# A fused four-stage kernel on one core: a new order of its head, with the mixed weights made in 32 products of 32 rows and 64 columns

## The chip, the cores and the metric

The kernel runs on one core of one Trainium2 chip. The metric is the device time of one execution in microseconds (us); the median of three runs is used.

## The reference, cut to what matters

The input x is [16 batches, 128, 128], and each batch has a row of 8 condition values, `cond_8`. Four residual stages follow one another:

```python
x = x + L0(x)   # per batch: one expert of 8 (argmax of cond), up/gate/down, silu, hidden 256
x = x + L1(x)   # base linear + 8 rank-16 adapters, mixed per batch by cond
x = x + L2(x)   # linear with w_bot[b] = sum_g cond[b, g] * weight[g] * mask, plus bias
x = x + L3(x)   # top-2 of 8 experts per batch (gelu, hidden 512), weighted, plus a shared expert
```

The linears of stages L1 and L2 depend on the batch through `cond_8` alone, so their 16 weight matrices per stage can be made before x is touched.

## The kernel before, in words

All work is written by hand per engine, with semaphores between the engines; each engine executes its own list in order.

**The head.** SP loads `cond_sb`, `lora_sb` and `w2_sb` (lines 258 to 260), ACT's queue loads `cond_rep` (cond repeated over the partitions), `small_sb` and x (385 to 387). TensorE (PE) first multiplies zeros (`warm`, 443 and 458). VectorE (DVE) finds the top 8 of each batch (632 to 637); a small product carries the first expert numbers to one row, `at_row` (461, 652), from which SP reads the addresses of the L0 experts and loads them into a ring of 10 slots (266). DVE makes `bs_w`, the adapters' second factor times cond (656), then `y_delta` (662), then works out by 26 small instructions, nearly all chained, which of 32 slots each (batch, expert) pair takes (`payload`, 667 to 707).

PE meanwhile makes the L1 weights: four products of 128 rows and 512 columns (`prepare1`, 452), which ACT copies out (397) and GpSimd (POOL) adds to the base weight (353, `lin1`). Then it makes the mixed L2 weights: 16 products of 64 rows and 128 columns (480), two of them side by side on the two halves of the array's rows; ACT copies them out in four pieces (402) and POOL multiplies by the mask in 16 pieces (361, `lin2`). Only then comes the first batch of stage L0 (`upgate0(0)`, 490), behind it a product that spreads `payload` over the partitions (508), which waits for all of ACT's copies, and then the other batches. DVE copies `slot_row` and `w_col` out of that product (722, 723), and SP and POOL wait for them (303, 348).

**The rest.** Each batch of L0 is 4 products for up and gate (490), silu on ACT (408), a multiply on DVE (714) and 2 products for down (498). After 16 batches come L1 and L2 for four groups (523, 530, and DVE's 735), and the split of x into a high part (ACT 414) and a low part (DVE 741). L3 then runs through a fixed list of units (`ORDER`); its weights are split into two parts by POOL first: the shared expert (365, 367) and then 12 pairs of slots ("duos", 375 and 378, three pieces each). All L3 products run as pairs of high and low parts (544, 554, 561, 588, 603, 612).

**Queues.** SP issues the ring loads, the shared expert's weights (300), the duo loads (272) and the solo loads (281) in one order; a ring slot is loaded again when its batch is done (265), a duo's raw buffer when POOL has split it (271).

Of the kernel before, what the change touches and what calls it, by code (L numbers as in the profile page):

```python
# [22 lines left out]
P = 128  # L23
B = 16
E = 8
# [21 lines left out]
HALF = P // 2  # L47
J = HALF // E
QUADS = 2
RANKED = 12  # L50
BASE1, MASK2, DELTA, BIAS1, BIAS2 = 0, P, 2 * P, 2 * P + J, 2 * P + J + 1
# [10 lines left out]
EYE, IOTA, EVENS, BELOW, EARLIER, NUMBER, SLOT = E, E + B, 2 * E + B, 2 * E + 2 * B, 2 * E + 2 * B + E * E, \  # L62
    2 * E + 3 * B + E * E, 2 * E + 3 * B + E * E + 1
COND = SLOT + SLOTS

SLOTS0 = 10
FREE = 2
PAIRS = 3
# [50 lines left out]
def build_kernel(nc, xT, cond, condT, lora, small, w2, experts0, experts3, shared, out):  # L119
    ctx = ExitStack()  # L120
    with ctx:
# [3 lines left out]
        def sem(name):  # L125
# [13 lines left out]
        w2_sb = sb("w2_sb", [P, E, P])  # L139
# [20 lines left out]
        pw_rest = sb("pw_rest", [B, K])  # L160
        pw_all = sb("pw_all", [B, K])
# [5 lines left out]
        reached = sb("reached", [B, E, B])  # L167
        even_odd = sb("even_odd", [B, 2, E])
        in_front = sb("in_front", [B, 2, E, E])
        starts = sb("starts", [B, 2, E])  # L170
        evens = sb("evens", [B, 1])
        even_slot = sb("even_slot", [B, E])
        odd_slot = sb("odd_slot", [B, E])
        is_odd = sb("is_odd", [B, E])
        shift = sb("shift", [B, E])
        shifted = sb("shifted", [B, E])
# [4 lines left out]
        payload = sb("payload", [B, 3, K, SLOTS])  # L181
        slot_row = sb("slot_row", [1, 2 * SLOTS], U32)
# [7 lines left out]
        mix_raw = sb("mix_raw", [P, QUADS, 2, GB, B, J])  # L190
# [25 lines left out]
        route = sem("route")  # L216
# [3 lines left out]
        chosen_done, rank_mm, payload_done, slots_mm, slots_done = (  # L220
            sem("chosen_done"), sem("rank_mm"), sem("payload_done"), sem("slots_mm"), sem("slots_done"))
        ydelta_done, bsw_done = sem("ydelta_done"), sem("bsw_done")
        prep_mm, prep_copied = sem("prep_mm"), sem("prep_copied")
# [33 lines left out]
        def _(sp):  # L257
            sp.dma_start(cond_sb[:, :], cond).then_inc(cond_in, 16)
            sp.dma_start(lora_sb[:, :], lora).then_inc(lora_in, 16)
            sp.dma_start(w2_sb[:, :, :], w2).then_inc(w2_in, 16)  # L260
# [45 lines left out]
            for b in range(SLOTS0 + 2, B):  # L306
                load0(b)
# [33 lines left out]
        def _(pool):  # L341
# [4 lines left out]

            pool.wait_ge(small_in, 16)
            pool.wait_ge(slots_done, 1)
            for q in range(G):
                pool.wait_ge(prep_copied, q + 1)  # L350
# [19 lines left out]
            for j in range(DUOS):  # L370
# [3 lines left out]
                for n in range(3):  # L374
                    pool.tensor_copy(duo_hi[:, j % HALVES, piece(n)], raw_duo[:, j % RAWS, piece(n)])\  # L375
# [66 lines left out]
        def _(pe):  # L442
# [26 lines left out]
            for q in range(G):  # L469
                prepare1(q)  # L470
# [417 lines left out]
```

## Time and profile before

| | us |
|---|---|
| median of three runs | 153.79 (153.7 to 154.18) |
| the profiled execution's own time | 154.21 |
| its span, first to last instruction | 152.2 |
| time around the span | 2.0 |

The profiled execution lies 0.42 us above the median of the runs. In the span PE is busy 97%, DVE 72%, POOL 61% and ACT 47%; the granted TensorE clock reads 1.00 of full speed on average.

In the rows, PE is a product, PEld a load of its weights, and SPq and ACTq are DMA issues on the queues of SP and ACT. L12 is line 12 of the kernel. An fp32 product leaves two records of a load and two of a product, so `x8` at line 490 are four products.

### The profile page before, as it was taken

To read this page: it belongs to the slowest core of one execution; us is meant where nothing else is said; L and a number is where in the kernel's file an instruction comes from. 1 tells how busy PE (TensorE), PEld (TensorE's weight loads), DVE (VectorE), ACT (ScalarE), POOL (GpSimd) and SP (SyncE) were. 2 spreads that over 40 slices of the span, in tenths; PEclk is the share of its full clock that TensorE was granted. 3 is DMA by queue.
4 is the path that set the end of the run, shared out by engine and by line. 5 is a ranking of instruction groups with operands and counts; after the bars stand their busy time and mean duration, and the time that the engine had idled before them with its cause. 6 is when DMAs were issued, how large, how long until landed. Compare 5 with 4: busy or idle time off the path is not lost.

```text
span 152.2 us, 3148 instructions
## 1 busy us (share of the span) xinstructions
PE 147.4 (97%) x1091; PEld 134.0 (88%) x1091; DVE 110.0 (72%) x229; ACT 71.6 (47%) x138; POOL 93.1 (61%) x101
## 2 busy tenths in 40 slices
PE   7999999999999999999999999999999999999992
PEld 2468999999976999899989999999989999999881
DVE  2984666666896686768875868876587886968772
ACT  3666444462374554544454354545425434346640
POOL 1002999999910006939994939995875999880000
PEclk9999999999999999999999999999999999999999
DMA  3999999971653667294297477086448047000052
GB/s 93 395 408 401 413 400 394 424 253 39 243 216 109 179 155 253 48 294 140 57 324 243 146 234 243 5 281 225 187 116 297 5 126 287 6 0 0 0 209 71
DMA packets 13919, 30.15 MB, mean 198 GB/s; under 512 B 1344, under 2 KB 8016, under 8 KB 13776
## 3 DMA queue, kind: packets, MB, share of 16 engines
q1 hardware_dynamic: 13472, 28.76, 54.4%
q10 hardware_dynamic: 432, 1.19, 2.2%
q8 instruction: 9, 0.15, 0.4%
q14 instruction: 6, 0.05, 0.2%
HBM read 24.71 MB, written 1.05 MB: 169 GB/s over the span
## 4 chain that ended last, share of the span: by engine, by line
PE 83%; DVE 7%; ACT 3%; POOL 3%; issue 2%; ACTq 0%; DVEq 0%; POOLq 0%
PE pair L554 21%; PE acc L603 10%; PE pair L544 9%; PE pair L490 9%; PE pair L561 8%; PE acc L588 6%; PE acc L498 5%; PE acc L612 5%; PE acc L445 3%; PE pair L452 2%; PE pair L523 2%; DVE hid L776 2%; DVE hid_lo L767 2%; POOL duo_lo L378 2%; DVE x_hl L741 2%; ACT hid_hi L438 2%
## 5 line engine op out<-in xcount | busy, mean ns | idle before, releaser
L378 POOL TENSOR_TENSOR duo_lo<-raw_duo,duo_hi 128x512 fp32r<-128x512 f32 x36 | 49.1, 1364 | 2.9
L767 DVE TENSOR_TENSOR hid_lo<-hid,hid_hi 128x512 fp32r<-128x512 f32 (+1 forms) x41 | 36.1, 883 | 17.8 <-ACT hid_hi L438 17.3
L438 ACT ACTIVATE hid_hi<-hid 128x512 fp32r<-128x512 f32 (+1 forms) x41 | 25.4, 622 | 44.0 <-DVE hid L776 41.1
L375 POOL CAST duo_hi<-raw_duo 128x512 fp32r<-128x512 f32 x36 | 28.4, 790 | 27.1 <-PE acc L603 27.1
L776 DVE TENSOR_TENSOR hid<-pair,act 128x512 f32<-128x512 f32 (+1 forms) x49 | 32.9, 673 | 5.6 <-PE pair L554 4.1
L554 PE MATMUL pair<-x_duo,duo_hi 128*128 128x256 f32 x192 | 35.1, 281 | 0.2 <-POOL duo_lo L378 0.2
L419 ACT ACTIVATE act<-pair 128x512 f32<-128x512 f32 x48 | 28.3, 590 | 9.6 <-PE pair L554 7.7
L554 PEld LDWEIGHTS pair<-x_duo,duo_hi 128*128 128x128 f32 x192 | 29.6, 188 | 0.9 <-issue 0.4
L554 PE MATMUL pair<-x_duo,duo_lo 128*128 128x256 f32 x96 | 26.8, 279 | 0.0
L544 PE MATMUL pair<-x_hl,shared_hi 128*128 128x512 f32 x64 | 20.5, 402 | 0.0
L554 PEld LDWEIGHTS pair<-x_duo,duo_lo 128*128 128x128 f32 x96 | 18.0, 188 | 0.0
L490 PE MATMUL pair<-x,ring 128*128 128x128 f32 x128 | 17.1, 277 | 0.0
L714 DVE SCALAR_TENSOR_TENSOR hid<-pair,ring,act 128x128 f32<-128x128 f32 x32 | 9.8, 346 | 8.5 <-PE pair L490 7.1
L490 PEld LDWEIGHTS pair<-x,ring 128*128 128x128 f32 x128 | 15.6, 192 | 0.2
L561 PE MATMUL pair<-x,raw_solo 128*128 x128 | 15.6, 275 | 0.0
L561 PEld LDWEIGHTS pair<-x,raw_solo 128*128 128x128 f32 x128 | 15.1, 192 | 0.3
L408 ACT ACTIVATE act<-pair,ring 128x128 f32<-128x128 f32 x32 | 10.0, 366 | 11.0 <-PE pair L490 11.0
L603 PE MATMUL acc<-hid_hi,duo_hi 128*128 128x256 f32 x48 | 14.2, 296 | 0.0
L603 PE MATMUL acc<-hid_hi,duo_lo 128*128 128x256 f32 x48 | 13.5, 282 | 0.0
L603 PE MATMUL acc<-hid_lo,duo_hi 128*128 128x256 f32 x48 | 13.5, 281 | 0.0
L544 PEld LDWEIGHTS pair<-x_hl,shared_hi 128*128 128x128 f32 x64 | 11.3, 189 | 2.0
L544 PE MATMUL pair<-x_hl,shared_lo 128*128 128x512 f32 x32 | 12.6, 394 | 0.0
(101 smaller groups left out, 200.6 us busy)
## 6 DMA issues: line engine op xcount, KB each, us to landing
raw_duo<-experts SPq DMA_DIRECT2D x12, 768.0 KB, 5.1
ring<-experts SPq DMA_DIRECT2D x16, 386.5 KB, 6.5
raw_solo<-experts SPq DMA_DIRECT2D x8, 768.0 KB, 4.7
x_duo<-x_hl SPq DMA_DIRECT2D x24, 128.0 KB, 3.8
x<-xT ACTq DMA_DIRECT2D x1, 1024.0 KB, 6.6
lora_raw<-x SPq DMA_DIRECT2D x4, 256.0 KB, 2.3
raw_solo<-shared SPq DMA_DIRECT2D x1, 768.0 KB, 10.9
out<-lora_raw SPq DMA_DIRECT2D x3, 256.0 KB, 3.1
```

The source lines that it names most:

```text
L375: pool.tensor_copy(duo_hi[:, j % HALVES, piece(n)], raw_duo[:, j % RAWS, piece(n)])\
L378: pool.tensor_tensor(duo_lo[:, j % HALVES, piece(n)], raw_duo[:, j % RAWS, piece(n)], duo_hi[:, j % HALVES, piece(n)].bitcast(F32), ALU.su ...
L408: act.activation(act0[:, b % FREE, c, :], pair[b % FREE][0][:, c * P:(c + 1) * P], ACT.Silu, bias=ring0[:, b % SLOTS0, BUP0 + c:BUP0 + c + ...
L419: act.activation(act3[:, u % PAIRS, :], pair[u % PAIRS][0][:, :], ACT.Gelu_apprx_tanh)\
L438: act.activation(hid_hi[:, k % SPLITS, at], hid3[:, u % PAIRS, at], ACT.Copy)\
L490: ins = pe.matmul(pair[b % FREE][half][:, c * P:(c + 1) * P], ring0[:, b % SLOTS0, base + c * P:base + (c + 1) * P], x[:, cols(b)], start= ...
L544: ins = pe.matmul(bank[:, :].rearrange("p (b n) -> p b n", n=P), w[:, at], x_hl[:, n * GB:(n + 1) * GB, h, :], start=(m == 0), stop=(m == 2))
L554: ins = pe.matmul(bank[:, i * N2:(i + 1) * N2], w[:, n % HALVES, at], x_duo[:, n % GATHERS, h, :], start=(m == 0), stop=(m == 2))
L561: ins = pe.matmul(bank[:, m * P:(m + 1) * P], raw_solo[:, n % RAWS, base + m * P:base + (m + 1) * P], x[:, cols(solo_batch[n])], start=Tru ...
L603: ins = pe.matmul(y, w[:, n % HALVES, at], v[:, k, i * N2:(i + 1) * N2], start=(part == 0 and i == 0 and m == 0), stop=(part == 1 and i == ...
L767: dve.tensor_tensor(hid_lo[:, k % SPLITS, at], hid3[:, u % PAIRS, at], hid_hi[:, k % SPLITS, at].bitcast(F32), ALU.subtract).then_inc(hid_ ...
L776: dve.tensor_tensor(hid3[:, u % PAIRS, at], pair[u % PAIRS][1][:, at], act3[:, u % PAIRS, at], ALU.mult).then_inc(mul_done, 1)
```

## The change

- **Loads.** `cond_rep` is no longer loaded: PE makes it from `cond_sb` with a small product (8 rows, 64 columns), ACT copies it out. `w2_sb` is loaded in two halves, ahead of x and `small_sb`, all on SP; ACT's queue keeps only `lora_sb`, behind a load of the exp table. `y_delta`'s pattern moves from `small_sb` into `w2_sb`.
- **DVE.** `y_delta` comes before `at_row`, and waits for the first half of `w2_sb`. The sorting takes a prefix sum and a predicated copy, fewer instructions, and comes behind `bs_w`. The weights of the top 2 are worked out on POOL.
- **PE.** Of eight `warm` products of 512 columns five are left, and two of 128 columns are added; the mixed L2 weights come before the L1 weights, as 32 products of 32 rows and 64 columns, four of them on the four quarters of the array's rows, into four banks. The `payload` product is one instead of two, and stands after `upgate0(3)`.
- **ACT.** Two of the four mixed banks are copied out before the L1 copies, and two between batches 0, 1 and 2 of L0.
- **POOL.** `lin1` and `lin2` no longer wait for `slots_done`; the mask takes 4 instructions of 512 elements in place of 16 of 128. The third piece of duo 1 waits for `hid_lo_done` 2.
- **SP.** The shared expert comes after 7 ring loads (10 before), and all ring loads come before the first duo.

The diff, cut to its core:

```diff
+TILES = 4
+ROWS = P // TILES
+J = ROWS // E
+KB = N // (B * J)
+MIXES = E // KB
+W2_HALF = J + E // 2 * P
...
-        prep = pair[2] + acc[:1]
-        mix = [[acc[1], pair[1][0]], [pair[1][1], pair[2][1]]]
-        cond_in, rep_in, lora_in = sem("cond_in"), sem("rep_in"), sem("lora_in")
-        small_in, w2_in = sem("small_in"), sem("w2_in")
+        prep = acc + pair[1]
+        mix = pair[1] + pair[2]
...
-            sp.dma_start(lora_sb[:, :], lora).then_inc(lora_in, 16)
-            sp.dma_start(w2_sb[:, :, :], w2).then_inc(w2_in, 16)
+            sp.dma_start(w2_sb[:, 0:W2_HALF], w2[:, 0:W2_HALF]).then_inc(w2_in[0], 16)
+            sp.dma_start(w2_sb[:, W2_HALF:], w2[:, W2_HALF:]).then_inc(w2_in[1], 16)
+            sp.dma_start(x[:, :], xT).then_inc(x_in, 16)
+            sp.dma_start(small_sb[:, :], small).then_inc(small_in, 16)
...
-            for b in range(4, SLOTS0):
-                load0(b)
-            sp.dma_start(shared_sb, shared).then_inc(shared_in, 16)
-            for b in range(SLOTS0, SLOTS0 + 2):
+            for b in range(4, B):
+                if b == SLOTS0 - 3:
+                    sp.dma_start(shared_sb, shared).then_inc(shared_in, 16)
                 load0(b)
             sp.wait_ge(slots_done, 1)
             duo_expert = values(mybir.EngineType.SP, slot_row[0:1, SLOTS:SLOTS + 2 * DUOS], E)
             load_duo(0)
...
+            pool.wait_ge(placed_done, 3)
+            pool.tensor_tensor(payload_sum[:, :, :], payload[:, :, 0, :], payload[:, :, 1, :], ALU.add)\
+                .then_inc(payload_done, 1)
...
-            for n in range(QUADS):
-                for h in range(2):
-                    pool.wait_ge(prep_copied, G + 2 * n + h + 1)
-                    for k in range(GB):
-                        at = (n * GB + k) * R + h * J
-                        mask = small_sb[:, MASK2 + at:MASK2 + at + J].unsqueeze(1).to_broadcast([P, B, J])
-                        ins = pool.tensor_tensor(lin2[:, :, at:at + J], mix_raw[:, n, h, k, :, :], mask, ALU.mult)
-                    ins.then_inc(lin2_done, 1)
+            for i in range(MIXES * TILES):
+                n, h = i // TILES, i % TILES
+                pool.wait_ge(mix_copied, i + 1)
+                at = slice(n * KB, (n + 1) * KB)
+                dst = lin2[:, :, :].rearrange("p b (k h j) -> p h k b j", h=TILES, j=J)[:, h, at, :, :]
+                mask = small_sb[:, MASK2:MASK2 + P].rearrange("p (k h j) -> p h k j", h=TILES, j=J)[:, h, at, :]
+                pool.tensor_tensor(dst, mix_raw[:, n, h, :, :, :], mask.unsqueeze(2).to_broadcast([P, KB, B, J]),
+                                   ALU.mult).then_inc(lin2_done, 1)
...
+                    if j == 1 and n == 2:
+                        pool.wait_ge(hid_lo_done, 2)
...
-            rep = condT.unsqueeze(1).to_broadcast([2 * E, J, B])
-            act.dma_start(cond_rep[:, :], rep).then_inc(rep_in, 16)
-            act.dma_start(small_sb[:, :], small).then_inc(small_in, 16)
-            act.dma_start(x[:, :], xT).then_inc(x_in, 16)
+            act.preload_act_table(ACT.Exp)
+            act.dma_start(lora_sb[:, :], lora).then_inc(lora_in, 16)
...
+            act.wait_ge(ydelta_done, 1)
+            act.activation(cond_rep[:, :], pair[0][0][:, 0:B * J].rearrange("p (b j) -> p b j", j=J)[:, :, 0],
+                           ACT.Copy).then_inc(rep_done, 1)
             act.preload_act_table(ACT.Silu)
+            def mixed(i):
+                n, h = i // TILES, i % TILES
+                act.wait_ge(mix_mm, n + 1)
+                act.activation(mix_raw[:, n, h, :, :, :].rearrange("p k b j -> p (k b j)"), mix[i][:, :], ACT.Copy)\
+                   .then_inc(mix_copied, 1)
+            mixed(0)
+            mixed(1)
             for q in range(G):
                 act.wait_ge(prep_mm, q + 1)
-                act.activation(lora_raw[:, q * GB:(q + 1) * GB, :].rearrange("p b o -> p (b o)"), prep[q % 3][:, :],
-                               ACT.Copy).then_inc(prep_copied, 1)
-            for n in range(QUADS):
-                act.wait_ge(prep_mm, G + n + 1)
-                for h in range(2):
-                    act.activation(mix_raw[:, n, h, :, :, :].rearrange("p k b j -> p (k b j)"), mix[n][h][:, :],
-                                   ACT.Copy).then_inc(prep_copied, 1)
+                act.activation(lora_raw[:, q * GB:(q + 1) * GB, :].rearrange("p b o -> p (b o)"), prep[q][:, :],
+                               ACT.Copy).then_inc(lora_copied, 1)
...
+                if b < 2:
+                    mixed(2 + b)
...
             pe.wait_ge(zeros_set, 1)
-            warm(5)
+            warm(3)
+            warm(1, P)
+            pe.wait_ge(cond_in, 16)
+            pe.matmul(pair[0][0][:, 0:B * J].rearrange("p (b j) -> p b j", j=J), cond_sb[0:E, OF:OF + P],
+                      cond_sb[0:E, TURNED:TURNED + B].unsqueeze(2).to_broadcast([E, B, J]), start=True, stop=True)\
+              .then_inc(rep_mm, 1)
+            warm(1, P)
             pe.wait_ge(ones_set, 3)
             pe.wait_ge(at_diag_done, 1)
             pe.matmul(acc[1][:, 0:B], ones_b[:, :], at_diag[:, :], start=True, stop=True).then_inc(at_mm, 1)
             warm(1)
             pe.wait_ge(chosen_done, 1)
             pe.matmul(pair[0][1][0:B, 0:E], earlier_b[:, :], chosen_b[:, :], start=True, stop=True)
             pe.matmul(pair[0][1][0:B, E:2 * E], ones_b[:, 0:B], chosen_b[:, :], start=True, stop=True)\
               .then_inc(rank_mm, 1)
-            warm(2)
+            warm(1)
+            pe.wait_ge(ydelta_done, 1)
+            for k in range(E):
+                if k % (E // 2) == 0:
+                    pe.wait_ge(w2_in[k // (E // 2)], 16)
+                for h in range(TILES):
+                    rows = slice(h * ROWS, (h + 1) * ROWS)
+                    ins = pe.matmul(mix[k // KB * TILES + h][:, k % KB * B * J:(k % KB + 1) * B * J],
+                                    w2_sb[rows, J + k * P:J + (k + 1) * P],
+                                    y_delta[rows, :, :].rearrange("p b j -> p (b j)"), start=True, stop=True)
+                if k % KB == KB - 1:
+                    ins.then_inc(mix_mm, 1)
             for q in range(G):
-                prepare1(q)
-            pe.wait_ge(ydelta_done, 1)
-            pe.wait_ge(w2_in, 16)
-            for n in range(QUADS):
-                if n:
-                    pe.wait_ge(prep_copied, 2)
-                for k in range(GB):
-                    for h in range(2):
-                        rows = slice(h * HALF, (h + 1) * HALF)
-                        ins = pe.matmul(mix[n][h][:, k * P:(k + 1) * P], w2_sb[rows, n * GB + k, :],
-                                        y_delta[rows, :, :].rearrange("p b j -> p (b j)"), start=True, stop=True)
-                ins.then_inc(prep_mm, 1)
+                pe.wait_ge(bsw_done, q + 1)
+                if q >= FREE:
+                    pe.wait_ge(mix_copied, q - FREE + 1)
+                pe.matmul(prep[q][:, :], lora_sb[:, AS1:AS1 + P],
+                          bs_w[:, q * GB:(q + 1) * GB, :].rearrange("p b o -> p (b o)"),
+                          start=True, stop=True).then_inc(prep_mm, 1)
...
-            pe.wait_ge(route, RANKED)
+            pe.wait_ge(rank_done, 1)
             upgate0(0)
-            pe.wait_ge(payload_done, 3)
-            pe.wait_ge(prep_copied, 2 * QUADS + G)
-            for k in range(K):
-                ins = pe.matmul(prep[0][:, 0:3 * SLOTS].rearrange("p (v s) -> p v s", v=3), ones[:, :],
-                                payload[:, :, k, :], start=(k == 0), stop=(k == K - 1))
-            ins.then_inc(slots_mm, 1)
+            pe.wait_ge(lora_copied, G)
             for b in range(B):
                 if b + 1 < B:
                     upgate0(b + 1)
-                if b == FREE:
+                if b == SORTED:
+                    pe.wait_ge(payload_done, 1)
+                    pe.wait_ge(mix_copied, 3)
+                    pe.matmul(pair[2][0][:, 0:3 * SLOTS], ones[:, :], payload_sum[:, :, :].rearrange("b v s -> b (v s)"),
+                              start=True, stop=True).then_inc(slots_mm, 1)
+                if b == SORTED + FREE:
                     pe.wait_ge(slots_done, 2)
...
+            dve.wait_ge(rep_mm, 1)
+            dve.wait_ge(w2_in[0], 16)
+            dve.tensor_tensor(y_delta[:, :, :], pair[0][0][:, 0:B * J].rearrange("p (b j) -> p b j", j=J),
+                              w2_sb[:, 0:J].unsqueeze(1).to_broadcast([P, B, J]), ALU.mult).then_inc(ydelta_done, 1)
             dve.wait_ge(at_mm, 1)
             dve.tensor_copy(at_row[:, :], acc[1][0:1, 0:B]).then_inc(at_done, 1)
+            dve.tensor_tensor(onehot[:, :, :], top_at[:, 0:K].unsqueeze(2).to_broadcast([B, K, E]),
+                              cond_sb[:, IOTA:IOTA + E].unsqueeze(1).to_broadcast([B, K, E]), ALU.is_equal)\
+               .then_inc(onehot_done, 1)
+            dve.wait_ge(onehot_done, 1)
+            dve.tensor_tensor(chosen_b[:, :], onehot[:, 0, :], onehot[:, 1, :], ALU.add).then_inc(chosen_done, 1)
+            dve.wait_ge(rank_mm, 1)
+            dve.tensor_copy(count_i[:, :], pair[0][1][0:B, E:2 * E]).then_inc(route, 1)
+            dve.tensor_copy(rank_n[:, :], pair[0][1][0:B, 0:2 * E]).then_inc(rank_done, 1)
+            dve.wait_ge(exp_done, 1)
+            dve.reciprocal(inv[:, 0:1], expsum[:, :]).then_inc(inv_done, 1)
+            dve.wait_ge(rep_done, 1)
...
+            dve.tensor_tensor_scan(starts[:, :], parts[:, 0:2 * E], none[:, :], 0.0, ALU.add, ALU.add).then_inc(route, 1)
...
-            dve.wait_ge(slots_mm, 1)
-            dve.tensor_copy(slot_row[:, :], prep[0][0:1, 0:2 * SLOTS]).then_inc(slots_done, 1)
-            dve.tensor_copy(w_col[:, :], prep[0][:, 2 * SLOTS:3 * SLOTS]).then_inc(slots_done, 1)
             for b in range(B):
                 if b + 1 < B:
                     hidden0(b + 1)
+                if b == SORTED:
+                    dve.wait_ge(slots_mm, 1)
+                    dve.tensor_copy(slot_row[:, :], pair[2][0][0:1, 0:2 * SLOTS]).then_inc(slots_done, 1)
+                    dve.tensor_copy(w_col[:, :], pair[2][0][:, 2 * SLOTS:3 * SLOTS]).then_inc(slots_done, 1)
```

## Rows read from the trace of the kernel before

**Rows 1.** The page, busy time of each engine (share of the span) xinstructions

```profile
PE 147.4 (97%) x1091; PEld 134.0 (88%) x1091; DVE 110.0 (72%) x229; ACT 71.6 (47%) x138; POOL 93.1 (61%) x101
```

**Rows 2.** Busy time by stretch: length, then each engine (instructions), clock, DMA share, GB/s

```profile
20.00:30.00 10.00, 10.00 (x92) 10.00 (x92) 6.54 (x23) 4.70 (x16) 9.92 (x16) 1.00 1.03 409
```

**Rows 3.** Chain that ended last, in order of time: start us, us, what

```profile
4.25 0.97 PE acc L445 x2
...
10.79 2.08 ACT mix_raw L402 x4
...
13.00 0.65 PE pair L508 x4
13.65 1.09 PE pair L490 x8
14.74 0.45 PE acc L498 x4
15.19 0.89 PE pair L490 x8
```

**Rows 4.** Timeline of the head, DVE and SP: start us, us, what [idle before]

```profile
3.39 0.15 DVE L649 TENSOR_TENSOR chosen_b<-onehot 16x8 bf16<-16x8 f32 x1
...
3.69 0.16 DVE L652 CAST at_row<-acc 1x16 uint32<-1x16 f32 x1 [0.15 <-PE acc L461]
3.78 2.48 DVE L656 SCALAR_TENSOR_TENSOR bs_w<-lora_sb,cond_rep 128x512 f32<-128x512 f32 x4
...
4.58 5.85 SPq L266 DMA_DIRECT2D ring<-experts  x10
...
6.19 0.27 DVE L662 TENSOR_TENSOR y_delta<-cond_rep,small_sb 128x128 f32<-128x128 f32 x1
```

**Rows 5.** DMA issues: out<-in, count, KB each, us from issue to landing

```profile
x<-xT ACTq DMA_DIRECT2D x1, 1024.0 KB, 6.6
...
w_sb<-w SPq DMA_DIRECT2D x1, 512.0 KB, 3.9
...
lora_sb<-lora SPq DMA_DIRECT2D x1, 128.0 KB, 2.3
```

**Rows 6.** Timeline of the L1 products, loads and products of one record each, line 452

```profile
5.86 0.34 PEld L452 LDWEIGHTS pair<-bs_w,lora_sb 128*128 128x128 f32 x1 [0.52 <-DVE bs_w L656]
...
6.71 0.34 PEld L452 LDWEIGHTS pair<-bs_w,lora_sb 128*128 128x128 f32 x1 [0.52 <-issue]
...
7.34 0.19 PEld L452 LDWEIGHTS acc<-bs_w,lora_sb 128*128 128x128 f32 x1 [0.29 <-issue]
...
7.77 0.19 PEld L452 LDWEIGHTS acc<-bs_w,lora_sb 128*128 128x128 f32 x1 [0.24 <-issue]
```

**Rows 7.** Timeline of the mixing products (L480) and of the loads behind payload's (L508)

```profile
10.02 0.27 PE L480 MATMUL acc<-y_delta,w_sb 64*128 64x128 f32 x1
...
10.13 0.27 PE L480 MATMUL acc<-y_delta,w_sb 64*128 64x128 f32 x1
...
13.19 0.30 PEld L508 LDWEIGHTS pair<-payload,ones 16*128 16x128 f32 x2
13.30 0.19 PEld L508 LDWEIGHTS pair<-payload,ones 16*128 16x128 f32 x1
```

**Rows 8.** Timeline of POOL's masks and splits, and of DVE's low parts

```profile
14.12 2.50 POOL L353 TENSOR_TENSOR lin<-lora_raw,small_sb 128x512 f32<-128x512 f32 x2 [11.31 <-DVE w_col L723]
...
19.03 6.68 POOL L361 TENSOR_TENSOR lin<-mix_raw,small_sb 128x128 f32<-128x128 f32 x16
...
27.19 3.45 POOL L367 TENSOR_TENSOR shared_lo<-raw_solo,shared_hi 128x1536 fp32r<-128x1536 f32 x1
...
40.78 0.68 DVE L741 TENSOR_TENSOR x_hl<-x,x_hl 128x512 fp32r<-128x512 f32 x1
40.82 1.79 POOL L378 TENSOR_TENSOR duo_lo<-raw_duo,duo_hi 128x512 fp32r<-128x512 f32 x1
...
42.04 1.12 DVE L741 TENSOR_TENSOR x_hl<-x,x_hl 128x512 fp32r<-128x512 f32 x1
```

More of the change, by code:

```diff
@@ L116, with build_kernel @@
 SUMMED = dict(zip(ORDER, itertools.accumulate(additions(unit) for unit in ORDER)))
-def build_kernel(nc, xT, cond, condT, lora, small, w2, experts0, experts3, shared, out):
+def build_kernel(nc, xT, cond, lora, small, w2, experts0, experts3, shared, out):
     ctx = ExitStack()
@@ L138, in build_kernel @@
         small_sb = sb("small_sb", [P, SMALL])
-        w2_sb = sb("w2_sb", [P, E, P])
+        w2_sb = sb("w2_sb", [P, J + E * P])
         shared_sb = raw_solo[:, 0, :]
@@ L166, in build_kernel @@
         rank_n = sb("rank_n", [B, 2 * E])
[L167 to L176, printed above, removed]
+        count_i = sb("count_i", [B, E], U32)
+        odd_i = sb("odd_i", [B, E], U32)
+        parts = sb("parts", [B, 2 * E + 1])
+        none = sb("none", [B, 2 * E])
+        starts = sb("starts", [B, 2 * E])
+        is_odd = sb("is_odd", [B, E], U32)
         slot_e = sb("slot_e", [B, E])
@@ L305, in _ @@
             load_duo(0)
-            for b in range(SLOTS0 + 2, B):
-                load0(b)
             load_duo(1)
@@ L345, in _, with weighed @@
             pool.tensor_copy(earlier_b[:, :], cond_sb[:, EARLIER:EARLIER + B]).then_inc(ones_set, 1)
+            step = [0]
+            def weighed(ins):
+                step[0] += 1
+                ins.then_inc(weigh, 1)
+                pool.wait_ge(weigh, step[0])
+            pool.wait_ge(inv_done, 1)
+            weighed(pool.tensor_scalar(probs[:, :], expd[:, 0:K], inv[:, 0:1], None, ALU.mult))
+            pool.tensor_tensor(pair_sum[:, :], probs[:, 0:1], probs[:, 1:2], ALU.add).then_inc(pair_done, 1)
+            pool.wait_ge(inv_done, 2)
+            weighed(pool.tensor_scalar(pw[:, :], probs[:, :], inv[:, 1:2], None, ALU.mult))
+            weighed(pool.tensor_scalar(pw_rest[:, :], pw[:, :], 1.0 - W_SCALE, None, ALU.mult))
+            weighed(pool.tensor_scalar(pw_part[:, :], pw[:, :], W_SCALE, None, ALU.mult))
+            weighed(pool.tensor_tensor(pw_all[:, :], pw_part[:, :], pw_rest[:, :], ALU.add))
+            pool.wait_ge(placed_done, 1)
+            weighed(pool.tensor_tensor(payload[:, 2, :, :], placed[:, :, :],
+                                       pw_all[:, :].unsqueeze(2).to_broadcast([B, K, SLOTS]), ALU.mult))
+            pool.wait_ge(placed_done, 3)
+            pool.tensor_tensor(payload_sum[:, :, :], payload[:, :, 0, :], payload[:, :, 1, :], ALU.add)\
+                .then_inc(payload_done, 1)
             pool.wait_ge(small_in, 16)
-            pool.wait_ge(slots_done, 1)
             for q in range(G):
-                pool.wait_ge(prep_copied, q + 1)
+                pool.wait_ge(lora_copied, q + 1)
                 base = small_sb[:, BASE1:BASE1 + P].unsqueeze(1).to_broadcast([P, GB, P])
@@ L432, in _ @@
                     if k >= SPLITS:
-                        act.wait_ge(down_done, [AT[x] for x in SPLIT_AT][k - SPLITS] + 1)
+                        act.wait_ge(down_done, [AT[other] for other in SPLIT_AT][k - SPLITS] + 1)
                     width = N // splits(unit)
@@ L442, in _, with warm @@
         def _(pe):
-            def warm(times):
+            def warm(times, columns=N):
                 for _ in range(times):
-                    pe.matmul(acc[0][:, :].rearrange("p (b n) -> p b n", n=P), zeros[:, :],
-                              zeros[:, :].unsqueeze(1).to_broadcast([P, GB, P]), start=True, stop=True)
-            def prepare1(q):
-                pe.wait_ge(bsw_done, q + 1)
-                if q >= len(prep):
-                    pe.wait_ge(prep_copied, q - len(prep) + 1)
-                pe.matmul(prep[q % 3][:, :], lora_sb[:, AS1:AS1 + P],
-                          bs_w[:, q * GB:(q + 1) * GB, :].rearrange("p b o -> p (b o)"),
-                          start=True, stop=True).then_inc(prep_mm, 1)
-            pe.wait_ge(zeros_set, 1)
-            warm(5)
+                    pe.matmul(acc[0][:, 0:columns].rearrange("p (b n) -> p b n", n=P), zeros[:, :],
+                              zeros[:, :].unsqueeze(1).to_broadcast([P, columns // P, P]), start=True, stop=True)
+            pe.wait_ge(zeros_set, 1)
+            warm(3)
[5 more added lines that the diff above has]
+            warm(1, P)
             pe.wait_ge(ones_set, 3)
@@ L690, in _ @@
-            chained(dve.tensor_tensor(even_slot[:, :], starts[:, 0, :], rank, ALU.add))
-            chained(dve.tensor_scalar(odd_slot[:, :], starts[:, 1, :], evens[:, 0:1], None, ALU.add))
-            chained(dve.tensor_tensor(is_odd[:, :], rank, even_odd[:, 0, :], ALU.is_ge))
-            chained(dve.tensor_tensor(shift[:, :], odd_slot[:, :], even_slot[:, :], ALU.subtract))
-            chained(dve.tensor_tensor(shifted[:, :], shift[:, :], is_odd[:, :], ALU.mult))
-            chained(dve.tensor_tensor(slot_e[:, :], even_slot[:, :], shifted[:, :], ALU.add))
@@ new lines, in _ @@
+            dve.tensor_tensor(is_odd[:, :], rank_n[:, 0:E], parts[:, 1:E + 1], ALU.is_ge).then_inc(route, 1)
+            dve.wait_ge(route, 8)
+            dve.tensor_tensor(slot_e[:, :], starts[:, 0:E], rank_n[:, 0:E], ALU.add).then_inc(route, 1)
+            dve.wait_ge(route, 10)
+            dve.copy_predicated(slot_e[:, :], is_odd[:, :], starts[:, E:2 * E]).then_inc(route, 1)
+            dve.wait_ge(route, 11)
+            dve.tensor_tensor(slot_ke[:, :, :], onehot[:, :, :], slot_e[:, :].unsqueeze(1).to_broadcast([B, K, E]),
+                              ALU.mult).then_inc(route, 1)
```

115 lines of the change are left out of this document (49 added, 66 removed).

## The prediction

> **What bounds the kernel now.** I read four views. The page's busy time comes first: the reader should see that TensorE is busy 97% of the span [rows 1]. The table by stretch then says where it is full: between 20 and 30 us PE is busy all 10.00 us, with the DMA engines full beside it at 409 GB/s [rows 2]. So what counts is when the unbroken stream of products begins. The chain in order of time gives that: ACT's four copies of the mixed weights hold it from 10.79 to 12.87, the `payload` product follows at 13.00, and from 13.65, the second batch of L0, the chain stays on PE, batch behind batch [rows 3]. Last, the timeline of the head tells what feeds it [rows 4, 6, 7]. A batch costs 0.89 for up and gate and 0.45 for down, 1.34 us together [rows 3]. Whatever lets the second batch begin earlier than 13.65 should come off the end, if the loads and POOL keep up.
>
> **Part by part: the new head on PE.**
>
> *Start of the mixing.* `y_delta` now waits for the first half of `w2_sb`. No row shows a half load. The nearest are `lora_sb`, 128 KB, issued second on SP at 1.23 and landed 2.3 later, at 3.5, and the whole `w_sb`, issued at 1.68 and landed 3.9 later, at 5.6 [rows 5]. Those are the bounds; in between 512 KB took 2.1 us, so 258 KB land near 4.0, which I take. `y_delta` is at most 0.27, `at_row` 0.16, `chosen_b` 0.15 and `onehot` about the same [rows 4]: `chosen_b` is ready near 4.8 instead of 3.54. One warm product (two took 0.97 [rows 3]) and the two rank products, some 0.1 by an estimate from `payload`'s steps in rows 7, put the first mixing product at 5.4. By the bounds it is 4.9 or 7.0.
>
> Behind that wait `at_row` ends near 4.4 instead of 3.85, and SP's first ring load goes out near 5.1 instead of 4.58 [rows 4]. I cost that at nothing: the same DMA engines are still busy with `w2_sb` and x until then, and x landed at 8.7 [rows 5].
>
> *The clock.* The granted clock reads 1.00 in the tables, but the spacing of equal records tells more: line 452's loads stand 0.85 apart from 5.86 to 6.71, 0.63 from there to 7.34, and 0.43 to 7.77 [rows 6]. That is 1.2 GHz up to about 7.0, and 2.4 GHz from there, after PE had worked almost from the start of the span with hardly a gap. I take the same moment for the new head.
>
> *The mixing.* Each of its records needs its own weights. Two tiles side by side advance one record every 0.11 (10.02 to 10.13) with 128 columns; the `payload` product, with 16 rows and only 96 columns, still loads every 0.11 (13.19 to 13.30) [rows 7]. So fewer rows and fewer columns did not shorten a step there. The old mixing has 16 such steps (8 products of 2 records, two tiles at a time), the new one 16 as well (8 of 2 records, four tiles at a time). I take 0.11 at 2.4 GHz and, from rows 6, twice that at 1.2. The bounds are 0.055 if 64 columns set the step, and 0.22 if four quarters load only two at a time. From 5.4 to 7.0 that makes 7.6 steps, and the other 8.4 take 0.9: the mixing ends at 7.9. The saving is its place, not its length.
>
> The Trainium skill agrees on the load (TensorE: Matmul & The Clock Gate, section LDWEIGHTS): it counts columns of the weights, so 32 rows of 128 columns take as long as 128 rows.
>
> *Behind it.* Four L1 products of 2 x 0.43 end at 11.35. DVE's four `bs_w`, 0.62 each, begin near 5.5 and are done by 8.0, one ahead of each product. ACT's copies, 0.52 apart where they follow one another (four in 2.08 [rows 3]), run two mixed, then four L1, from 8.1; the last starts behind the last L1 product and ends by 12.1. `upgate0(0)`, 0.89, ends at 12.25; so ACT's copies no longer stand on the path. The `payload` product, one of two records instead of two of two, costs 0.22. The stream is thus where it was at 13.65 by about 12.45: **1.2 us** earlier.
>
> **What I cost at nothing.** ACT's last two mixed copies, 0.52 each, stand between batches 0 to 2, where ACT is less than half busy (4.70 of 10.00 us [rows 2]). Were this cover gone, they would cost up to 1.0. DVE's 13 sorting instructions, near 0.2 each with their steps (0.15 to 0.16 long [rows 4]), and POOL's eight are done by about 11.5, and are now needed only after `upgate0(3)`, near 15. x and the first ring slot land by about 9.7, before 11.35. The ring loads take 0.97 each (396 KB at 409 GB/s [rows 2]) against 1.34 of work, and with the shared expert (1.9) ahead of the eighth, that lands near 18.4 and is needed at 20.7. The duos go out later on SP, behind all 16 ring loads, but arrive near 27, when POOL has just finished: its `lin1` is 5.0 (four of 1.25) from about 12, `lin2` between 5.0 (four at that size) and 6.7 (as before), the shared split 4.9 [rows 8], so 28.6 at the latest. POOL was first at its duos at 30.6.
>
> **The step to L3.** In the old run a low part on DVE takes 1.12 from 42.04, another of the same shape 0.68, and the long one ends 0.55 after POOL's last split of duo 1, which itself ran 1.79 until 42.6 [rows 8]. The two kept each other waiting. The new wait moves that split behind `hid_lo` 2, so DVE is free: **0.4 us**. If POOL is late after all, this is 0. Behind POOL's new wait stands its third piece of duo 1, and on SP the load of duo 3, both used several units later.
>
> **The sum.** 1.2 + 0.4 = 1.6 us. The profiled execution, 154.21 (152.2 of span and 2.0 around it), would become 152.6. It lies 0.42 above the median of the runs; from 153.79 the forecast is **152.2 us**.
>
> **Rivals.**
>
> *The columns set the step.* With 64 columns and four quarters at work, a step may take 0.11 at the lower clock and 0.055 at the higher. Then the mixing ends at 7.1, 0.8 earlier, and the time is 151.4. For it: with 128 columns load and columns cannot be told apart. Against it: the 96-column product at 0.11 [rows 7]. If the clock is up already at 5.4 as well, the mixing ends at 6.3 and the time is 150.6. The Trainium skill's page TensorEngine Tiling (Array Packing), Theoretical Speedup, has up to 4x for 32 rows against 2x for 64, which would halve the old 1.76 us of mixing to 0.88.
>
> *The clock rises later (slower).* The new head has three 512-column warm products fewer, it leaves PE idle near 4.0 to 4.8, and its mixing, if the loads pace it, streams only part of the time. If PE stays at 1.2 GHz, the mixing ends at 8.8 and each L1 product takes 1.71. With two of them at that rate the stream is at its old point at 15.0 instead of 13.65; less 0.4, that is 1.0 slower, 154.8; with all four it is 156.5. Each us by which the clock rises later costs 0.5 us, so the gain of 1.6 is gone if it rises after about 10.2. For it: PE needed until 7.0 with its denser start [rows 6]. Against it: most of the stretch from 5.4 on is still work.
>
> *Four quarters do not load together.* Then there are 32 steps of 0.11, the mixing ends at 9.7, and 1.8 of time is added to a gain of 1.6: 154.0. Against it: the old two halves share a step of 0.11 [rows 7].
>
> **How the numbers follow.** Forecast 0.45, columns 0.28, clock 0.18, loads apart 0.09. A measurement of this kernel can tell about 0.3%, 0.46 us, from no change. The first two are faster: 0.73. Of the clock's 0.18, 0.05 lies within 0.46, and most of the third: 0.11 the same; 0.16 slower. The range reaches from 150.8, which leaves out only the earliest clock, to 154.0, which leaves out the clock's dearer ends and some of the third. The forecast's own range is 151.8 to 152.9: a later half load costs up to 0.9, and the 0.4 may be missing.
>
> **What would show it.** Right: `mix` starts near 5.4 and advances one round of four tiles per 0.21, then 0.11; the records of the L1 products are 0.43 apart; the second batch of L0 begins near 12.2; L741 takes 0.68 four times; PE has no new gap from 15 to 34. Wrong: rounds of 0.055 or 0.22; L1 records 0.85 apart behind the mixing; a PE wait on `e0_in`, on `shared_done` or on ACT's copies; or a stream that begins earlier and still ends at the same time.

## The result, and the profile after

The changed kernel takes **156.83 us** (median of 4, 156.18 to 157.29) against 153.75 before (153.69 to 154.18). The ratio is 1.020, 95% interval 1.016 to 1.024: 3.1 us slower, where 152.2 was forecast and 154.0 was the upper end. The profiled execution took 156.54, with a span of 154.8 and 1.7 around it; that span is 2.6 longer than before.

The page, busy time of each engine (share of the span, instructions), answers to [rows 1]:

```profile
PE 149.9 (97%) x1122; PEld 136.4 (88%) x1122; DVE 109.1 (70%) x221; ACT 71.6 (46%) x139; POOL 94.7 (61%) x97
```

PE's share is the same 97%, so it has no new idle time: it is busy 2.5 us longer. The chain that ended last, in order of time (start us, us, what), shows where. It answers to [rows 3]; the mixing is now L506, the L1 weights L516, up and gate of L0 L526, the `payload` product L548, the linears of L1 L560:

```profile
4.04 0.23 DVE y_delta L681
...
5.39 3.62 PE pair L506 x64
9.02 3.71 PE acc L516 x4
12.73 1.97 PE pair L516 x4
14.70 1.85 PE pair L526 x16
...
19.23 0.39 PE pair L548 x2
19.62 0.64 PE acc L534 x4
...
37.10 3.57 PE pair L560 x32
...
45.76 0.69 DVE hid L803
...
51.54 1.31 DVE hid_lo L794
...
57.36 0.72 PE acc L640 x6
```

Three marks of the same chain of the kernel before, for the same work (first linear, first multiply of L3 on DVE, first down product of a duo):

```profile
34.71 3.57 PE pair L523 x32
...
43.75 0.68 DVE hid L776
...
54.95 0.71 PE acc L603 x6
```

The loss is complete where the linears begin: 37.10 against 34.71, 2.4 us. At DVE's first multiply of L3 it is 2.0, and at the first duo's down product 2.4 again. (The two traced executions are 2.3 us apart in time, the medians 3.1: the traced kernel before lies 0.4 above its median, the traced changed kernel 0.3 below.)

The timeline of the changed kernel, loads of the L1 weights as in [rows 6], then POOL and DVE at the step to L3 as in [rows 8]:

```profile
11.67 0.34 PEld L516 LDWEIGHTS pair<-bs_w,lora_sb 128*128 128x128 f32 x1 [0.52 <-issue]
12.52 0.34 PEld L516 LDWEIGHTS pair<-bs_w,lora_sb 128*128 128x128 f32 x1 [0.52 <-issue]
13.25 0.19 PEld L516 LDWEIGHTS pair<-bs_w,lora_sb 128*128 128x128 f32 x1 [0.39 <-issue]
13.68 0.19 PEld L516 LDWEIGHTS pair<-bs_w,lora_sb 128*128 128x128 f32 x1 [0.24 <-issue]
...
33.30 0.61 POOL L403 CAST duo_hi<-raw_duo 128x512 fp32r<-128x512 f32 x1 [7.12 <-DMA raw_duo<-experts]
...
49.55 0.69 DVE L794 TENSOR_TENSOR hid_lo<-hid,hid_hi 128x512 fp32r<-128x512 f32 x1 [0.70 <-ACT hid_hi L472]
...
51.00 1.29 POOL L406 TENSOR_TENSOR duo_lo<-raw_duo,duo_hi 128x512 fp32r<-128x512 f32 x1
...
51.54 1.30 DVE L794 TENSOR_TENSOR hid_lo<-hid,hid_hi 128x512 fp32r<-128x512 f32 x1 [0.70 <-ACT hid_hi L472]
```

The loads stand 0.85 apart up to 12.52 and 0.43 from 13.25: TensorE works at 1.2 GHz until about 13, where before it was at 2.4 GHz from about 7 [rows 6]. The whole mixing (16 rounds of 0.21), four of the eight L1 records and most of the fifth ran at the lower level. The granted clock reads 1.00 in all these stretches; only the spacing shows it.

### The profile page after: what moved, and what is told of

Its sections match the earlier page's. It is cut to its first block, busy times and chain, and to the rows that moved or that the text cites. A ratio compares the mean times of both kernels' runs of the same rounds, so it can differ in the third digit from the quotient of the medians.

```text
span 154.8 us, 3205 instructions
## 1 busy us (share of the span) xinstructions
PE 149.9 (97%) x1122; PEld 136.4 (88%) x1122; DVE 109.1 (70%) x221; ACT 71.6 (46%) x139; POOL 94.7 (61%) x97
## 4 chain that ended last, share of the span: by engine, by line
PE 83%; DVE 9%; ACT 2%; DMA 2%; issue 1%; SPq 0%; ACTq 0%; DVEq 0%
PE pair L591 21%; PE acc L640 10%; PE pair L526 9%; PE pair L598 9%; PE pair L581 8%; PE acc L625 5%; PE acc L534 5%; PE acc L649 5%; DVE hid L803 3%; DVE hid_lo L794 3%; PE acc L516 2%; ACT hid_hi L472 2%; PE pair L506 2%; PE pair L560 2%; DMA w_sb<-w 2%
## 5 line engine op out<-in xcount | busy, mean ns | idle before, releaser
L794 DVE TENSOR_TENSOR hid_lo<-hid,hid_hi 128x512 fp32r<-128x512 f32 (+1 forms) x41 | 38.6, 943 | 17.7 <-ACT hid_hi L472 17.3
L403 POOL CAST duo_hi<-raw_duo 128x512 fp32r<-128x512 f32 x36 | 29.1, 808 | 34.4 <-PE acc L640 19.9
L406 POOL TENSOR_TENSOR duo_lo<-raw_duo,duo_hi 128x512 fp32r<-128x512 f32 x36 | 48.2, 1338 | 2.9
L740 DVE SCALAR_TENSOR_TENSOR hid<-pair,ring,act 128x128 f32<-128x128 f32 x32 | 9.8, 347 | 13.1 <-PE pair L526 12.8
L526 PE MATMUL pair<-x,ring 128*128 128x128 f32 x128 | 16.8, 275 | 0.0
L526 PEld LDWEIGHTS pair<-x,ring 128*128 128x128 f32 x128 | 15.6, 192 | 0.5 <-issue 0.5
```

Of the source, the lines that this page charges most:

```text
L406: pool.tensor_tensor(duo_lo[:, j % HALVES, piece(n)], raw_duo[:, j % RAWS, piece(n)], duo_hi[:, j % HALVES, piece(n)].bitcast(F32), ALU.su ...
L526: ins = pe.matmul(pair[b % FREE][half][:, c * P:(c + 1) * P], ring0[:, b % SLOTS0, base + c * P:base + (c + 1) * P], x[:, cols(b)], start= ...
L794: dve.tensor_tensor(hid_lo[:, k % SPLITS, at], hid3[:, u % PAIRS, at], hid_hi[:, k % SPLITS, at].bitcast(F32), ALU.subtract).then_inc(hid_ ...
```

## The experiments

Three theories. **Form**: the mixing's products of 64 columns stream too little, and stand where the clock should rise. **Warm**: the missing warm products and the gaps ahead of 5.3 hold it down. **Steps**: the clock apart, only the number of steps counts.

The moment at which the clock rises is read from the spacing of the L1 or mixing records: one spacing lies between the two levels, and it is divided in proportion.

| run | products ahead of the full clock | 1.2 GHz until about | linears begin | median | ratio to before |
|---|---|---|---|---|---|
| before | 8 warm, L1 | 7.1 | 34.71 | 153.75 | |
| changed | 5 + 2 short warm, 64-column mixing, L1 | 13.1 | 37.10 | 156.83 | 1.020 |
| `e1_two_halves` | as changed, 128-column mixing | 8.4 | 34.92 | 155.13 | 1.0105 (1.0071 to 1.0138) |
| `e2_no_gaps` | 8 warm, 64-column mixing, L1 | 13.4 | 37.45 | 157.06 | 1.0229 (1.0199 to 1.026) |
| `e3_l1_first` | as changed, L1 ahead of the mixing | 8.9 | 35.95 | 155.96 | 1.0155 (1.0112 to 1.0197) |
| `e4_before_three_warm_fewer` | 5 warm, L1 | 8.5 | 35.11 | 154.28 | 1.0051 (1.0025 to 1.0077) |
| `e7_halves_64_columns` | as changed, 64-column mixing in 64 rows | 18 | 41.30 | 160.56 | 1.0438 (1.0387 to 1.049) |

Each ratio is to runs of the kernel before on the same chip (medians 153.4 to 153.7).

**Two halves again** (`e1_two_halves`, `e8_two_halves_again`):

```diff
-TILES = 4
+TILES = 2
```

> The changed kernel with one number changed: the mixed weights come from 16 products of 64 rows and 128 columns, two tiles side by side, in the new order and with the new few warm products. In the changed kernel the L1 products' records stand 0.85 us apart up to 12.5, and the clock is up only near 13.1; before it was near 7.0. Theory 'form' (products of 64 columns stream too little to bring the clock up): here the records of the mixing are full again, the clock rises near 7 to 9, the L1 products follow at 0.43, and the median falls by 2 to 3 us, to about 154. Theory 'warm' (the missing warm products and the gaps before 5.3 hold the clock down): no change, the clock still rises near 13 and the median stays near 156.8. Theory 'cost of the products alone' (clock as it is, only the number of steps counts): 16 steps as before, no change.

Timeline, loads of the mixing (L506) and of the L1 weights (L516):

```profile
5.38 3.32 PEld L506 LDWEIGHTS pair<-y_delta,w_sb 64*128 64x128 f32 x32 [0.44 <-issue]
8.82 0.30 PEld L516 LDWEIGHTS acc<-bs_w,lora_sb 128*128 128x128 f32 x2
9.35 0.19 PEld L516 LDWEIGHTS acc<-bs_w,lora_sb 128*128 128x128 f32 x1 [0.24 <-issue]
9.78 0.19 PEld L516 LDWEIGHTS acc<-bs_w,lora_sb 128*128 128x128 f32 x1 [0.24 <-issue]
```

One number changed, and the L1 products run 0.43 apart; the linears begin 2.2 earlier than in the changed kernel, and the median is 1.7 lower, a little less than expected. So *form*, not *warm* or *steps*. The mixing itself took nearly the same time (3.4 us instead of 3.6): the step stayed at 0.21 and fell to 0.11 only for its last two, when the clock rose near 8.4. That is still later than the 7.1 of the kernel before, which stays ahead.

> The kernel with two halves once more, for a second look at its clock, since its six times lie between 154.29 and 155.81. If the clock rises at another moment in another execution, this trace shows it at another place than near 8.8, and its time differs by about half of that shift; if the clock rises at the same place, the spread has another cause.

The loads are 0.43 apart from 9.91 on, the clock rises near 9.5 instead of 8.4, and the span is 0.5 longer (153.1 against 152.6), about half of the shift. The moment moves between executions and the time with it.

**No gaps** (`e2_no_gaps`), full warm products ahead of the mixing:

```diff
-            warm(3)
-            warm(1, P)
+            warm(4)
...
-            warm(1, P)
+            warm(1)
...
-            warm(1)
+            warm(2)
             pe.wait_ge(chosen_done, 1)
```

> The changed kernel with warm products of 512 columns in its three gaps before 5.3 us (eight of 512 columns in all, as in the kernel before), the mixing still 32 products of 64 columns. Theory 'warm': the clock rises near 7, the mixing's rounds of four go from 0.21 to something shorter, the L1 products run at 0.43 apart, and the median falls by 2 to 3 us. Theory 'form': the clock still rises near 13, the median stays within 0.5 us of 156.8.

Timeline, loads of the L1 weights:

```profile
12.93 0.34 PEld L515 LDWEIGHTS pair<-bs_w,lora_sb 128*128 128x128 f32 x1 [0.52 <-issue]
13.60 0.19 PEld L515 LDWEIGHTS pair<-bs_w,lora_sb 128*128 128x128 f32 x1 [0.33 <-issue]
14.03 0.19 PEld L515 LDWEIGHTS pair<-bs_w,lora_sb 128*128 128x128 f32 x1 [0.24 <-issue]
```

Eight warm products do not help: the clock is as late as in the changed kernel. *Warm* falls for the changed kernel.

**L1 first** (`e3_l1_first`): the loop over the L1 products stands ahead of the mixing loop, ACT's copies in the same order, `prep = acc + pair[0]`.

> The changed kernel with the four L1 products ahead of the 32 mixing products (banks and copies follow), all else as changed. Theory 'form': from 5.7 on PE streams 512 columns per record again, so the clock rises near 7 to 10, and the mixing then runs at 2.4 GHz: its round of four takes 0.11 us if the loads set it, 0.055 if the columns do. The median falls by 1.5 to 3 us. Theory 'warm': the clock rises as late as in the changed kernel, near 13, and L1 products and mixing take 1.71 and 0.21 again; median near 156.8 or above.

Timeline, the L1 weights (L504), then the mixing (L514):

```profile
5.92 1.22 PE L504 MATMUL acc<-bs_w,lora_sb 128*128 128x512 f32 x1 [0.45 <-DVE bs_w L700]
...
8.65 0.32 PEld L504 LDWEIGHTS pair<-bs_w,lora_sb 128*128 128x128 f32 x1 [0.52 <-issue]
9.21 0.19 PEld L504 LDWEIGHTS pair<-bs_w,lora_sb 128*128 128x128 f32 x1 [0.24 <-issue]
...
11.02 2.01 PE L514 MATMUL pair<-y_delta,w_sb 32*128 32x64 f32 x64
```

With 512-column products from 5.9 on the clock is up near 9. The mixing takes 2.0 us at 2.4 GHz for 16 rounds, as the old form did. The median falls by 0.9 only, less than expected. The L1 products wait for `bs_w` until 5.92, where those of the kernel before began at 5.00. ACT's two mixed copies also hold back the second batch, by about 0.3: its products could have followed at 13.95 and began at 14.23.

**Fewer warm products before** (`e4_before_three_warm_fewer`): `warm(5)` to `warm(3)`, `warm(2)` to `warm(1)`.

> The kernel before with five warm products of 512 columns instead of eight (three of the first five, one of the last two), nothing else. Theory 'warm': the clock rises later than 7.0, the L1 products take 1.71 longer, and the time grows by 1 to 3 us. Theory 'form': the L1 products, which start near 4.8, bring the clock up near 7 to 8.5 all the same; the time stays within 0.5 us of 153.75.

Timeline, loads of the L1 weights:

```profile
7.88 0.34 PEld L452 LDWEIGHTS acc<-bs_w,lora_sb 128*128 128x128 f32 x1 [0.52 <-issue]
8.60 0.19 PEld L452 LDWEIGHTS pair<-bs_w,lora_sb 128*128 128x128 f32 x1 [0.39 <-issue]
9.03 0.19 PEld L452 LDWEIGHTS pair<-bs_w,lora_sb 128*128 128x128 f32 x1 [0.24 <-issue]
```

The clock comes near 8.5, about 1.4 later, and the median is 0.6 to 0.8 higher, between the two expectations. Where full products follow, warm products do count, though for a fifth to a quarter of the loss.

**Columns or tiles** (`e7_halves_64_columns`): on top of two halves,

```diff
+                    for c in range(2):
+                        at = k % KB * B * J + c * B // 2 * J
```

with 64 columns per product.

> The kernel with two tiles of 64 rows, but each of its 16 products cut into two of 64 columns: 32 products, 64 columns as in the changed kernel, 64 rows as in the kernel with two halves. Theory 'columns' (products of 64 columns leave the array half empty between two loads): 32 steps of 0.21 at the lower clock, 6.9 us of mixing, the clock still down at its end and up only some us into the L1 products; the median is 3 us or more above the changed kernel's 156.8. Theory 'tiles' (it is the four tiles of 32 rows that keep the clock down): the clock rises near 9 as with two halves, the rest of the mixing runs at 0.11, and the median lies between 155 and 157.5.

Timeline, the mixing (L508), then loads of the L1 weights (L519):

```profile
5.42 7.15 PE L508 MATMUL pair<-y_delta,w_sb 64*128 64x64 f32 x64
...
16.92 0.34 PEld L519 LDWEIGHTS pair<-bs_w,lora_sb 128*128 128x128 f32 x1 [0.52 <-issue]
17.78 0.29 PEld L519 LDWEIGHTS pair<-bs_w,lora_sb 128*128 128x128 f32 x1 [0.52 <-issue]
18.31 0.19 PEld L529 LDWEIGHTS pair<-x,ring 128*128 128x128 f32 x1 [0.24 <-issue]
```

With the tiles of `e1_two_halves` and only the columns halved, 32 steps of 0.22 run at 1.2 GHz from end to end, and the clock is up near 18. So the 64 columns are enough to keep the clock down, without tiles of 32 rows: the step is as long with 64 columns as with 128 (0.22 and 0.21), and carries half as many. Whether tiles of 32 rows with more columns would do it too was not tried.

**The titled part alone, in the old place** (`e12_before_four_quarters`): the kernel before with 32 products of 32 rows and 64 columns behind its L1 products.

> The kernel before with the titled part of the change alone: in the old place, behind the L1 products, the mixed weights come from 32 products of 32 rows and 64 columns, four quarters of the rows side by side, and POOL's mask in four instructions. Theory 'the load sets the step': at 2.4 GHz 16 rounds of four, 0.11 each, 1.8 us as before; ACT's four copies can start only behind the last product, 0.5 to 0.7 later than before, so the payload product and the stream move by as much: 0.4 to 0.8 us slower than the kernel before. Theory 'columns set the step': 0.055 a round, 0.9 us of mixing, and the time is 0.1 to 0.5 us below the kernel before. If the clock falls again during the thin mixing: 1 us or more slower.

Timeline, one tile's products:

```profile
8.74 0.27 PE L475 MATMUL acc<-y_delta,w_sb 32*128 32x64 f32 x1
...
8.86 0.27 PE L475 MATMUL acc<-y_delta,w_sb 32*128 32x64 f32 x1
```

Chain in order of time:

```profile
10.66 2.07 ACT mix_raw L399 x4
...
12.87 0.65 PE pair L503 x4
```

A round of four takes 0.11, and 16 rounds 1.9: no shorter, no longer. The clock, already up near 5.3 in this execution, did not fall. Median 153.44 against 153.53, ratio 0.9993 (0.9968 to 1.0018): unchanged. The cost of ACT's later copies is there in the trace: from the first mixing product (8.58) to the `payload` product (12.87) it is 4.29, against 3.42 in the kernel before, 0.9 more. In this execution the earlier clock hides it (linears at 34.59 against 34.71); why the median does not show it stays open. So the 32 products did harm only where they preceded the full clock.

**POOL's wait** (`e5_no_pool_wait`): `pool.wait_ge(hid_lo_done, 2)` left out.

> The changed kernel without POOL's new wait for hid_lo 2 (the third piece of duo 1 is split as soon as its buffer is there). Theory 'moved stall' (the wait only moves the collision of POOL and DVE, from the low parts of x near 44 to the third hid_lo at 51.5, which took 1.30 instead of 0.69): POOL's third piece runs at about 42.9 to 44.8, one low part on DVE takes about 1.1, the hid_lo takes 0.69 again, and the median stays within 0.5 us of 156.8. Theory 'the wait helps': 0.4 us or more slower. Theory 'the wait hurts' (it is part of the 3 us): 0.5 us or more faster.

Timeline, POOL's third piece of duo 1 and DVE:

```profile
44.69 1.30 POOL L404 TENSOR_TENSOR duo_lo<-raw_duo,duo_hi 128x512 fp32r<-128x512 f32 x1
...
44.72 1.81 DVE L766 TENSOR_TENSOR x_hl<-x,x_hl 128x512 fp32r<-128x512 f32 x1
...
52.89 0.69 DVE L792 TENSOR_TENSOR hid_lo<-hid,hid_hi 128x512 fp32r<-128x512 f32 x1 [0.70 <-ACT hid_hi L470]
```

157.04, ratio 1.0198 (1.0145 to 1.025): no change from the changed kernel's 1.020. The collision is a low part of x again (1.81, done 0.54 after POOL's split beside it), and the third `hid_lo` is back at 0.69: the wait only chose the victim. The Trainium skill (Advanced Engine Details and Errata, VectorE Performance Modes, its note on the second Vector SBUF port) says that this port is shared with GpSimd, and that GpSimd instructions and Vector instructions that use two ports block each other. Whether DVE's subtraction is one of those no run shows; that it is held up beside POOL's split the rows do show.

**Versions meant to beat both.** `e6_l1_first_dense`: L1 first, `bs_w` made earlier, 512-column warm products in the gaps, the mixed banks away from batches 0 and 1.

> A version meant to beat both: the changed kernel with the L1 products first again, their bs_w made earlier (about 4.0 instead of 5.1), 512-column warm products in the gaps before them, then the 32 mixing products, in banks that keep ACT's copies off batches 0 and 1. Theory 'form': the clock is up near 7, the L1 products end near 9.5, the mixing takes 1.8 (16 steps of 0.11), the second batch starts near 12.4 instead of 13.65, the payload product costs 0.6 in the stream, and the median is about 0.5 to 0.8 below the kernel before, near 153.0. Theory 'warm or place': if the clock is late here too, it is 155 or more.

154.85, ratio 1.0074 (1.0046 to 1.0103): slower than the kernel before. Its loads turn from 0.85 to 0.43 apart between 8.62 and 9.31, not near 7, though PE is busy from 1.0. Ahead of its L1 products it has one warm product fewer than the kernel before (seven), and the small product of `cond_rep` at 2.8; whether either is the cause was not tried.

`e9_before_copies_off_path`: the kernel before with the mixed banks in `acc` and `pair[2]`, two of ACT's copies between batches, the `payload` product after `upgate0(3)`.

> The kernel before, its dense start and its order of the products kept, with two things of the changed kernel that do not touch the clock: the mixed weights go to banks that batches 0 and 1 do not need, with two of ACT's four copies between those batches, and the payload product stands after upgate0(3); POOL's lin1 waits for the payload instead of slots_done. Theory: the clock rises near 7 as before, the second batch starts near 12.5 instead of 13.65, the payload product (two products here) costs about 0.6 to 0.8 in the stream, and the median falls by 0.3 to 0.6 us. If the head's gain is given back elsewhere: within 0.3 us of the kernel before.

Timeline, the L1 products (L456) and the mixing (L484), then the chain in order of time:

```profile
4.69 3.60 PE L456 MATMUL pair<-bs_w,lora_sb 128*128 128x512 f32 x8
8.22 1.05 PE L484 MATMUL acc<-y_delta,w_sb 64*128 64x128 f32 x14
```

```profile
33.27 3.57 PE pair L532 x32
...
48.01 0.79 issue
48.80 1.64 PE pair L563 x12
...
54.65 0.71 PE acc L612 x6
```

The median is 153.84 against 153.62, ratio 1.0011 (0.9982 to 1.0039): no gain. The linears begin 1.4 earlier than in the trace of the kernel before, but that is hardly the edit's doing. In this execution the clock was up near 4.4 instead of 7.1, and all eight L1 records took 3.6. From the first mixing product to the linears it is 25.05 (8.22 to 33.27), against 25.13 before (9.58 to 34.71): the copies off the path gained about 0.9, and the `payload` product cost about 0.8 in the stream. At the first duo's down product the 1.4 has become 0.3, because PE waits 0.79 ahead of that duo's products. The wait is for the gather of x: the second of its two copies was issued at 45.24 and landed at 48.71, and the product began at 48.80; POOL's splits for this duo were long done.

`e11_copies_off_path_pool_wait`: the same with POOL's wait.

> The kernel before with ACT's copies off the path (as in the run of that name, where the products of L1 began at 33.27 instead of 34.71 but the first duo waited 0.79 at 48.0 and nothing was left in the time), and with the changed kernel's wait of POOL's third piece of duo 1 for hid_lo 2. Theory 'both bounds': the low part of x that took 1.15 takes 0.68, the gather of x for the first duo goes out 0.4 earlier, and the median falls to 0.3 to 0.5 us below the kernel before. Theory 'the collision moves': the third hid_lo takes 1.3 and gives the 0.4 back; within 0.3 us of the kernel before.

153.67, ratio 1.0009 (0.9986 to 1.0032). The wait ahead of the first duo is 0.90 there, and ends the same way (copy landed at 48.38, product at 48.47). No version was faster than the kernel before.

**The changed kernel again** (`e10_changed_again`):

> The changed kernel once more, one look. If its spread (156.18 to 157.29) is the moment at which the clock rises, the records of the L1 products turn from 0.85 to 0.43 apart at another place than near 13.1, and the time moves by about half the shift. In no case should the clock be up before the mixing ends near 9.

Timeline, loads of the L1 weights:

```profile
11.72 0.34 PEld L516 LDWEIGHTS pair<-bs_w,lora_sb 128*128 128x128 f32 x1 [0.52 <-issue]
12.57 0.19 PEld L516 LDWEIGHTS pair<-bs_w,lora_sb 128*128 128x128 f32 x1 [0.52 <-issue]
13.01 0.19 PEld L516 LDWEIGHTS pair<-bs_w,lora_sb 128*128 128x128 f32 x1 [0.24 <-issue]
```

The spacing turns at 12.57 instead of near 13.1, and the linears begin at 36.86 instead of 37.10: half of the shift, as expected. The whole span is only 0.1 shorter (154.7 against 154.8), so the spread of the times has other causes too.

## Why the prediction was wrong, step by step

**The step that failed is the clock**: "I take the same moment for the new head". PE stayed at 1.2 GHz until about 13 instead of 7. The mixing ended at 9.0 instead of 7.9, and the four L1 products took 5.7 instead of 3.44: 3.3 us. The rival "the clock rises later" had this, with its place and its cause ("its mixing, if the loads pace it, streams only part of the time"). I gave it 0.18, because "most of the stretch from 5.4 on is still work". That was the mistake: I had just worked out that the load sets the step and that fewer columns do not shorten it, and still counted steps with half of the columns as full work.

The rival's price was 154.8 for two L1 products at the lower level and 156.5 for four. About two and a half came, which is 155.2 by that price; the measured 156.8 is more, mainly for three reasons that follow: the `payload` product, the traces against the medians, and the step to L3.

**The `payload` product** was sized at 0.22. In the stream it costs 0.39 and makes the down product behind it 0.64 instead of 0.45: 0.58 in all, 0.36 more.

With these two terms the forecast at the linears, 1.2 earlier, becomes 1.2 - 3.3 - 0.36 = 2.5 later; measured 2.4.

**The trace that the forecast was read from** had a late clock. Of four traces with the head of the kernel before, it rises near 7.1 in this one and near 5.3, 4.4 and 4.2 in `e12_before_four_quarters`, `e9_before_copies_off_path` and `e11_copies_off_path_pool_wait`; and the execution lies 0.4 above its median. So the medians are further apart (3.1) than the two traces (2.3).

**The step to L3.** The 0.4 came as forecast: the low part that took 1.12 [rows 8] ran in 0.69, and the loss at DVE's first multiply of L3 is 2.0 instead of 2.4. It was given back six us later, where the third `hid_lo` takes 1.30 beside POOL's moved piece. I had looked at what the piece delays on POOL and on SP, not at what it meets on DVE.

**The premise of the sum**, that what begins earlier "should come off the end", holds only in part: where the stream ran 1.4 earlier (`e9_before_copies_off_path`) the gain shrank to 0.3 at the first duo, which waited for its gather of x. Whether the 1.2 would have come off in full with the clock as I took it, no run shows.

**What was right.** The half load landed at 3.9 (forecast 4.0), the mixing began at 5.33 (5.4). A round takes 0.21 at 1.2 GHz, and 0.11 at 2.4 (`e3_l1_first`, `e12_before_four_quarters`): the load sets it, so the rivals "columns" and "four quarters do not load together" both fall. Up to 4x for 32 rows, as the Trainium skill has it (TensorEngine Tiling (Array Packing), Theoretical Speedup), shows in no run here: at 2.4 GHz, from the first record to the product behind, 64 records of 32 rows took 1.94 us (`e3_l1_first`), and 32 records of 64 rows 1.99 in the kernel before. ACT's copies and the sorting left the path, and PE has no gap between 15 and 34. POOL was at its duos later than I had it (33.3, behind a wait of 7.1 for the load, which landed at 33 and not at 27); PE did not wait for its splits at the first duo.

## What to carry to other kernels

Before products are moved to the front of a kernel, work out how full each step is while TensorE is still at its lower clock: here products whose loads set the step, with half of the columns, kept it at 1.2 GHz, and everything behind them paid. Put such products behind full ones: in the old place the same 32 products left the median where it was. And read the clock from the spacing of equal records, since the table showed full speed throughout.

## What the runs showed that I had not expected

- The moment of the rise differs between executions with the same start: 7.1 in the kernel before, 5.3 to 4.2 in three versions of it that begin alike.
- A 16-row product between 128-row ones costs 0.58 us for two records, where the same two alone would be 0.22 by their step.
- A POOL split and a DVE subtraction of low parts that meet seem to take turns. In the changed kernel DVE's takes 0.69 alone, and 0.9 to 1.8 when POOL's began first, always ending about 0.55 after it. Where DVE began first (76.98) it takes 0.69, and POOL's 1.76 instead of 1.28.
